# A decoder layer on one core: cross-attention scores from rounded keys and doubled queries

## What is computed

```
x = x + attn(layernorm(x))                        # Wq Wk Wv Wo, scores / 16
x = x + xattn(layernorm(x), ctx, mask)            # 77 keys, scores / 4, masked
x = x + ffn(layernorm(x))                         # 1024 slots
# xattn:
q = split(Q @ Wq.T + bq); k = split(K @ Wk.T + bk); v = split(V @ Wv.T + bv)
score = where(mask == 0, -inf, einsum('bhqd,bhkd->bhqk', q, k) * scale)
out   = einsum('bhqk,bhkd->bhqd', softmax(score), v)   ...   out @ Wo.T + bo
# ffn:
logits = xn @ se.T; dispatch = softmax over tokens; combine = softmax over slots
slots = dispatch.T @ xn; processed = gelu(slots @ w1) @ w2; out = combine @ processed
```

## Time and profile before

| | us |
|---|---|
| median of 3 runs (lowest, highest) | 1778.03 (1777.96, 1778.81) |
| profiled execution: its own time | 1779.52 |
| its span, first to last instruction | 1777.7 |
| one pass of the loop, of 13 | 105.37 |

### The profile page before, as it was taken

One profiled execution on the slowest core, in us unless ns is written; L12 is line 12 of the kernel. 1 busy time (PEld: TensorE's weight loads), 2 busy tenths in 40 slices (PEclk: granted clock), 3 DMA queues, 4 the chain that ended last, 5 costly groups with the idle time before them and its releaser, 6 DMA issues.

```text
span 1777.7 us, 40856 instructions
## 1 busy us (share of the span) xinstructions
PE 1739.7 (98%) x17306; PEld 1574.4 (89%) x17306; DVE 1161.5 (65%) x2307; ACT 1018.4 (57%) x1775; POOL 438.9 (25%) x351
## 2 busy tenths in 40 slices
PE   8899999999999999999999999999999999999998
PEld 7778898898989889898998989889898988989988
DVE  4657576676766668576675767667676666765453
ACT  4446566565565656556566656656656565655553
POOL 2103131322222223132222223222222213222232
PEclk9999999999999999999999999999999999999999
DMA  5000000000000000000000000000000000000000
GB/s 162 10 1 10 1 10 8 10 8 1 16 1 10 7 9 9 1 10 7 10 8 1 16 2 10 7 10 7 1 16 2 10 7 10 8 1 7 1 7 7
DMA packets 20853, 19.67 MB, mean 11 GB/s; under 512 B 9921, under 2 KB 19777, under 8 KB 20289
## 3 DMA queue, kind: packets, MB, share of 16 engines
q1 hardware_dynamic: 20672, 17.06, 3.5%
HBM read 12.86 MB, written 4.19 MB: 10 GB/s over the span
## 4 chain that ended last, share of the span: by engine, by line
PE 84%; ACT 5%; DVE 5%; issue 4%; POOL 2%; DMA 0%; POOLq 0%; SPq 0%; DVEq 0%; ACTq 0%
PE ps L465 21%; PE ps L466 19%; PE ps L467 19%; PE ps L590 3%; PE ps L573 2%; PE ps L553 2%; PE ps L775 2%; PE ps L700 2%; PE ps L620 2%; PE ps L843 1%; PE ps L665 1%; PE ps L766 1%; POOL h_lo L1446 1%; PE ps L872 1%; ACT L1034 1%
## 5 line engine op out<-in xcount | busy, mean ns | idle before, releaser
L1446 POOL TENSOR_TENSOR h_lo<-h_f,h_hi 128x512 fp32r<-128x512 f32 x256 | 336.8, 1323 | 1052.8 <-DVE h_hi L1329 1052.8
L465 PE MATMUL ps<-sl_hi,w_hi 128*128 128x256 f32 x1024 | 304.9, 298 | 5.4 <-DVE sl_lo L1088 2.9
L465 PE MATMUL ps<-w_hi,h_hi 128*128 128x256 f32 x1024 | 301.0, 294 | 5.5 <-POOL h_lo L1446 5.3
L466 PE MATMUL ps<-w_hi,h_lo 128*128 128x256 f32 x1024 | 290.1, 283 | 0.0
L467 PE MATMUL ps<-w_lo,h_hi 128*128 128x256 f32 x1024 | 289.9, 283 | 0.0
L466 PE MATMUL ps<-sl_hi,w_lo 128*128 128x256 f32 x1024 | 288.8, 282 | 0.0
L467 PE MATMUL ps<-sl_lo,w_hi 128*128 128x256 f32 x1024 | 288.7, 282 | 0.0
L465 PEld LDWEIGHTS ps<-sl_hi,w_hi 128*128 128x128 f32 x1024 | 194.4, 190 | 28.9 <-ACT h_f L1034 14.2
L1329 DVE CAST h_hi<-h_f 128x512 fp32r<-128x512 f32 x256 | 175.4, 691 | 67.0 <-ACT h_f L1034 66.2
L1034 ACT ACTIVATE h_f<-ps 128x512 f32<-128x512 f32 x256 | 151.2, 598 | 104.6 <-PE ps L467 103.6
L465 PEld LDWEIGHTS ps<-w_hi,h_hi 128*128 128x128 f32 x1024 | 196.2, 192 | 15.0 <-POOL h_lo L1446 11.3
(11 more groups left out here) (213 smaller groups left out, 4229.6 us busy)
## 6 DMA issues: line engine op xcount, KB each, us to landing
x<-in_x SPq DMA_DIRECT2D x16, 256.0 KB, 2.7
out<-acc SPq DMA_DIRECT2D x16, 256.0 KB, 2.2
g_w<-in_w SPq DMA_DIRECT2D x2, 1024.0 KB, 12.1
cx<-in_ctxT SPq DMA_DIRECT2D x16, 77.0 KB, 2.0
g_wqk<-in_wqk SPq DMA_DIRECT2D x1, 1024.0 KB, 6.4
g_se<-in_se SPq DMA_DIRECT2D x1, 1024.0 KB, 8.6
biases<-in_bias SPq DMA_DIRECT2D x1, 640.0 KB, 4.8
mk_i<-in_mask SPq DMA_DIRECT2D x16, 38.5 KB
```

The lines of the kernel that those rows point to most:

```text
L465: te.matmul(o, lhs[0], rhs[0], start=first, stop=False)
L466: te.matmul(o, lhs[1], rhs[0], start=False, stop=False)
L1446: Q_.tensor_tensor(h_lo[:, part, :], h_f[:, part, :], h_hi[:, part, :].bitcast(f32), ALU.subtract)\
```

## The change

Cross-attention scores are now made as self-attention's are. `kv` writes the keys once (`k2`, padded to 78 columns, the padding set to zero once). VectorE doubles them (`k2_d`, step `k2d`), ScalarE rounds them (`k2_hi`, step `k2h`), VectorE makes `k2_lo` (step `k2l`). The queries go through `q2d`, `q2h` and `q2s` the same way. `scores2` has 32 f32r products of 78 columns in place of 16 float32 ones of 77; `shifted2` has for each e eight f32r products in place of four float32 ones. The mask is 312 columns wide. To make room, `pt2` lies in the memory of `pt`: `before_in_pt` makes each Exp wait for the value product of the one before it in the ring. `g_se` moves to the memory where `g_wqk` was, so that its load waits until `wqk_lo` is made. GpSimd splits `w2` in four instructions instead of one. All tables of the order are new, and `START` has 224 idle products where it had 197.

```diff
+CP = 78
...
-    kv_ps=1, km2=1, v2_sb=1, mk=3, q2_ps=1, q2_sb=1,
+    kv_ps=1, k2_ev=1, k2_d=1, k2_h=1, k2_lo=1, v2_sb=1, mk=3, q2_ps=1, q2_ev=1, q2_d=1, q2_h=1, q2_sb=1,
...
@@ -46,34 +47,35 @@
 
 ORDER = dict(
-        m.lt.0 l.outer.3.0 d.kv m.dispatch.0 l.outer.3.1 c.xt.1 m.slots.0 l.comb.3 d.xt.2 c.k c.q d.q2 c.v
-        m.hidden.0.0 d.scores2.0 m.hidden.0.1 m.hidden.0.2 d.mt2.0 m.hidden.0.3 m.lt.1 l.combine.3 d.shifted2.0
...
+        m.lt.0 l.outer.3.0 d.kv m.dispatch.0 l.outer.3.1 c.xt.1 l.comb.3 m.slots.0 d.xt.2 c.k c.q d.q2 m.hidden.0.0
+        c.v m.hidden.0.1 m.hidden.0.2 d.scores2.0 m.hidden.0.3 m.lt.1 d.mt2.0 l.combine.3 d.shifted2.0 m.outer.0.0
...
-    d.kv c.xt1 d.xt2 d.q2 d.mt2.0 c.mt.0 d.pv2.0 d.mt2.1 c.pv.0 d.tr2.0 d.pv2.1 d.ob2.0 c.mt.1 d.tr2.1 c.pv.1 d.ob2.1
+    d.kv c.xt1 d.xt2 d.q2 d.mt2.0 c.mt.0 d.pv2.0 d.tr2.0 d.mt2.1 c.pv.0 d.ob2.0 d.pv2.1 c.mt.1 d.tr2.1 c.pv.1 d.ob2.1
...
-    "d.xt2": ("xt2_lo", 1), "c.xt1": ("xt1_lo", 1), "d.xt3": ("xt3_lo", 1), "d.kv": ("v2_sb", 1), "d.q2": ("q2_sb", 1),
+    "d.xt2": ("xt2_lo", 1), "c.xt1": ("xt1_lo", 1), "d.xt3": ("xt3_lo", 1), "d.kv": ("v2_sb", 1), "d.q2": ("q2_ev", 1),
...
+def before_in_pt(name, batch):
+
+    at = QUAD_USERS.index(f"{name[0]}{batch}{name[1:]}")
+    for token in reversed(QUAD_USERS[:at]):
+        head, step, *k = token.split(".")
+        if step in ("quad", "oct"):
+            return ("pv" if step == "quad" else "pv2", int(k[0]) + 1), int(head[1:])
+    return None
...
-        pt = sb("pt", [P, R, NT, S])
+        r_pt = region(8 * KB)
+        pt = at("pt", [P, R, NT, S], f32, r_pt)
...
-        km2 = sb("km2", [P, 2, C, CTX])
+        k2 = sb("k2", [P, C, CP])
+        r_q2s, r_k2l = region(4 * KB), region(4 * Q * CP)
+        q2_d, q2s = at("q2_d", [P, Q, S], f32, r_q2s), at("q2s", [P, Q, S], f32r, r_q2s)
+        k2_d, k2_lo = at("k2_d", [P, Q, CP], f32, r_k2l), at("k2_lo", [P, Q, CP], f32r, r_k2l)
+        k2_hi = sb("k2_hi", [P, Q, CP], f32r)
+        q2_hi = at("q2_hi", [P, Q, S], f32r, r_xd)
         v2z = sb("v2z", [CTX, H, VW])
-        r_pt2 = region(8 * KB)
-        pt2 = at("pt2", [CTX, R, 2, S], f32, r_pt2)
+        pt2 = at("pt2", [CTX, R, 2, S], f32, r_pt)
...
-        g_se = at("g_se", [P, NS, D], f32, r_pt2)
+        g_se = at("g_se", [P, NS, D], f32, r_lg)
...
-                    pe.wait_ge(s["km2"], nth("km2", a, 1))
+                    pe.wait_ge(s["k2_lo"], nth("k2_lo", a, 1))
                     pe.wait_ge(s["mk"], nth("mk", a, 3))
                 for i in range(R):
                     one = slice(32 * i, 32 * i + 1)
-                    te.matmul(ps[:, 1 + i, 0:4 * CTX], ones[one, :], mk_r[one, :, :].rearrange("p u c -> p (u c)"),
+                    te.matmul(ps[:, 1 + i, 0:4 * CP], ones[one, :], mk_r[one, :, :].rearrange("p u c -> p (u c)"),
                               start=True, stop=False)
                 for e in range(2):
                     for t in range(NT):
-                        at = (2 * e + t) * CTX
-                        for i in range(R):
-                            rows = slice(32 * i, 32 * i + 32)
-                            last = te.matmul(ps[:, 1 + i, at:at + CTX], q2[rows, c, t * P:(t + 1) * P],
-                                             km2[rows, e, c, :], start=False, stop=(e, t) == (1, NT - 1))
+                        at = (2 * e + t) * CP
+                        for keys, end in ((k2_hi, False), (k2_lo, (e, t) == (1, NT - 1))):
+                            for i in range(R):
+                                rows = slice(32 * i, 32 * i + 32)
+                                last = te.matmul(ps[:, 1 + i, at:at + CP], q2s[rows, 2 * c + e, t * P:(t + 1) * P],
+                                                 keys[rows, 2 * c + e, :], start=False, stop=end)
...
-                    for i in range(R):
-                        rows = slice(32 * i, 32 * i + 32)
-                        te.matmul(ps[0:CTX, 1 + i, e * S:(e + 1) * S], km2[rows, e, c, :], q2[rows, c, :],
-                                  start=True, stop=False)
+                    for keys, first in ((k2_hi, True), (k2_lo, False)):
+                        for i in range(R):
+                            rows = slice(32 * i, 32 * i + 32)
+                            te.matmul(ps[0:CTX, 1 + i, e * S:(e + 1) * S], keys[rows, 2 * c + e, 0:CTX],
+                                      q2s[rows, 2 * c + e, :], start=first, stop=False)
...
+                if n == 3:
+                    act.wait_ge(s["q2_sb"], nth("q2_sb", a, 1))
...
             def ex(a, n):
 
                 act.wait_ge(s["st_ps"], nth("st_ps", a, n + 1))
-                if n:
-                    act.wait_ge(s["pv"], nth("pv", a, n))
+                before = before_in_pt(f"c.quad.{n}", a)
+                if before:
+                    (signal, k), b = before
+                    act.wait_ge(s[signal], nth(signal, b, k))
...
             def q2_step(a):
 
                 act.wait_ge(s["q2_ps"], nth("q2_ps", a, 1))
+                if later(a):
+                    act.wait_ge(s["q2_d"], nth("q2_d", a - 1, 1))
                 for c in range(C):
                     last = nc.scalar.activation(q2[:, c, :], ps[:, 0, c * S:(c + 1) * S], ACT.Identity,
                                                 scale=XATTN_SCALE, bias=bcol[:, 2, c:c + 1])
-                last.then_inc(s["q2_sb"], 1)
+                last.then_inc(s["q2_ev"], 1)
+
+            def q2h_step(a):
+                act.wait_ge(s["q2_d"], nth("q2_d", a, 1))
+                copy(q2_hi[:, :, :], q2_d[:, :, :]).then_inc(s["q2_h"], 1)
+
+            def k2h_step(a):
+                act.wait_ge(s["k2_d"], nth("k2_d", a, 1))
+                copy(k2_hi[:, :, :], k2_d[:, :, :]).then_inc(s["k2_h"], 1)
...
             def ex2(a, c):
 
                 act.wait_ge(s["st2_ps"], nth("st2_ps", a, c + 1))
-                if not c and not later(a):
-                    act.wait_ge(s["i_sps"], 2 * ND)
-                if c:
-                    act.wait_ge(s["pv2"], nth("pv2", a, c))
+                before = before_in_pt(f"d.oct.{c}", a)
+                if before:
+                    (signal, k), b = before
+                    act.wait_ge(s[signal], nth(signal, b, k))
...
-                    for e in range(2):
-                        last = V.tensor_scalar(km2[:, e, c, :], ps[:, 0, D + c * CTX:D + (c + 1) * CTX],
-                                               half[:, e:e + 1], bk2m[:, e, c:c + 1], ALU.mult, ALU.add)
-                last.then_inc(s["km2"], 1)
+                    last = V.tensor_scalar(k2[:, c, 0:CTX], ps[:, 0, D + c * CTX:D + (c + 1) * CTX], bk2c[:, c:c + 1], None,
+                                           ALU.add)
+                last.then_inc(s["k2_ev"], 1)
                 V.tensor_tensor(v2z[:, :, 0:HD], ps[0:CTX, 0, 0:D].rearrange("p (h d) -> p h d", h=H),
                                 bv2[0:CTX, :].rearrange("p (h d) -> p h d", h=H), ALU.add).then_inc(s["v2_sb"], 1)
+
+            def q2d_step(a):
+
+                dve.wait_ge(s["q2_ev"], nth("q2_ev", a, 1))
+                if later(a):
+                    dve.wait_ge(s["st2_ps"], nth("st2_ps", a - 1, C))
+                twice(q2_d, q2).then_inc(s["q2_d"], 1)
+
+            def q2s_step(a):
+
+                dve.wait_ge(s["q2_h"], nth("q2_h", a, 1))
+                V.scalar_tensor_tensor(q2s[:, :, :], q2_hi[:, :, :].bitcast(f32), cols[:, NMASK:NMASK + 1], q2_d[:, :, :],
+                                       ALU.mult, ALU.add).then_inc(s["q2_sb"], 1)
+
+            def k2d_step(a):
+
+                dve.wait_ge(s["k2_ev"], nth("k2_ev", a, 1))
+                if later(a):
+                    dve.wait_ge(s["st2_ps"], nth("st2_ps", a - 1, C))
+                twice(k2_d, k2).then_inc(s["k2_d"], 1)
+
+            def k2l_step(a):
+                dve.wait_ge(s["k2_h"], nth("k2_h", a, 1))
+                minus(k2_lo[:, :, :], k2_d[:, :, :], k2_hi[:, :, :]).then_inc(s["k2_lo"], 1)
 
             def mask(a):
 
                 dve.wait_ge(s["mask_in"], nth("mask_in", a, 32))
                 if later(a):
                     dve.wait_ge(s["ex2"], nth("ex2", a - 1, C))
-                V.tensor_scalar(mk_r[:, :, :], mk_i[:, :].unsqueeze(1).broadcast_to([P, 2 * NT, CTX]), 0.0, MASKED,
+                V.tensor_scalar(mk_r[:, :, :], mk_i[:, :].unsqueeze(1).broadcast_to([P, 2 * NT, CP]), 0.0, MASKED,
...
             def mx2_step(a, c):
 
                 dve.wait_ge(s["s2_ps"], nth("s2_ps", a, c + 1))
-                V.tensor_reduce(mx2[:, c, :, :], ps[:, 1:1 + R, 0:4 * CTX].rearrange("p i (u c) -> p i u c", u=2 * NT), AX,
+                V.tensor_reduce(mx2[:, c, :, :], ps[:, 1:1 + R, 0:4 * CP].rearrange("p i (u c) -> p i u c", u=2 * NT)[:, :, :, 0:CTX], AX,
...
+            Q_.memset(k2[:, :, CTX:CP], 0.0).then_inc(s["i_vz"], 1)
+            Q_.memset(mk_i[:, CTX:CP], 0).then_inc(s["i_vz"], 1)
...
```

(6 more changed lines are left out.)

234 lines of the change are left out of this document (116 added, 118 removed).

## The result

The changed kernel takes 1796.53 us (median of 4 runs, 1795.63 to 1797.51) where the kernel before, on the same chip, takes 1778.42: a ratio of 1.0097, 95% interval 1.0085 to 1.0109. Predicted were 1770.9 us and 1761 to 1782. The profiled execution has a span of 1795.3 us, 17.6 more than before.

The account below looks back on a forecast made before the run. TensorE was taken to bound the kernel, busy 104.78 of 105.37 us a pass. Terms +0.6 - 11.2 + 7.0 - 3.5 = -7.1 us gave 1770.9 us on the median's scale, range 1761 to 1782.

Parts of the forecast that it names:

- Products: TensorE's cross-attention products: scores2 slightly dearer, +0.6 us in all; shifted2 0.35 us shorter, 32 times, -11.2 us.
- the +0.6 us in sum: scores2 on TensorE: eight sets at 0.12 us, 0.96 in place of 0.94, +0.02 each over 32.
- The rival with dear short products: In scores2, f32r products of 78 columns stream at four times their columns: +7.7 us, 1778.0 us; 12 in 100.
- Queries in time: Ahead of scores2.0: the new query chain ends within 0.1 us of being wanted, cost 0, without margin.
- The late-queries rival: Query sum or shuffle loses 1.0 us a pass, delaying scores2.0: +13 us in the loop, 1783.9 us; 13 in 100.
- the 3.2 us of added VectorE work: New shuffles, sum and low part per batch, on VectorE's 72.07 us a pass: as a sum they cost nothing.
- The next link: From second maxima transposes to shifted2.0: VectorE 0.2 us late, set against the 0.18 wait for `h_lo` that goes: 0.
- Since TensorE has no slack in the loop, 26 of the 32 count in full: Of 32 savings of 0.35 us in shifted2, the loop's 26 count fully: -9.1 to -11.2 us, -11.2 taken.
- Prologue: Before the loop: +7.0 us of waiting allowed by added idle products, -3.5 us from the earlier `xh_a`.
- The 7.0 us of idle products: In the prologue, 27 more idle products on TensorE at 0.26 us each mean +7.0 us more waiting.
- The closed waits: Rival: the new order also closes TensorE's remaining loop waits, 0.59 plus about 0.2 us a pass, -10, 1761 us; 15 in 100.

Follow-up runs that it names:

- i_narrow_q2: Changed kernel with the new VectorE and ScalarE steps on q2 done on 32 of 256 columns from the second batch on; 1794.87 us, 1.0090.
- o_old_products_moves: Products and probability tiles of the kernel before, run in the order of j_both; 1788.52 us, 1.0054.
- j_both: c_bias_back with second-half steps reordered on VectorE and ScalarE, and the first hidden group's last high part made on ScalarE; 1774.69 us, 0.9975.
- c_bias_back: Changed kernel with the bias of x1 on GpSimd put back ahead of the hidden layer's four low parts; 1786.99 us, 1.0038.
- d_keep_later: Changed kernel with VectorE's copy of the residual moved from ahead of the second shift to behind the MoE accumulation; 1795.42 us, 1.0088.
- b_old_tables: Changed kernel's products and tiles in the order tables and rings of the kernel before, six new steps put in; 1860.83 us, 1.0456.

## Why the prediction was wrong

- **Products: right.** A scores2 takes 1.18 us, so the +0.6 us in sum didn't come; a shifted2 takes 0.87 against 0.92 predicted. The rival with dear short products is out: eight sets of 78 columns pass in 0.96 us (473.94 to 474.90).
- **Queries in time: right**, and with more margin than predicted: `q2s` ends at 473.33, scores2.0 starts at 473.72. The late-queries rival is out; `q2s` took 1.28 us in the mean, 1.29 at most. That the 3.2 us of added VectorE work cost nothing was right as well (i_narrow_q2, o_old_products_moves).
- **The next link: the step that failed.** The prediction put 0.2 us of new wait in front of shifted2.0 and set it against the 0.18 for `h_lo`: 0. Measured are 0.54 us more from combine.3 to shifted2.0 (2.14 to 1.60). The term that was mis-sized is one of the three operations of 0.4 to 0.7 between maximum and shift: the last cast, 0.97 beside GpSimd's low part. By the rows (an estimate, see j_both) that is about 0.44 of the 0.54, and the chain without it 0.1. The 0.18 for `h_lo` did go, as predicted, but it doesn't cover 0.54. And this was the only link that was followed. The four others, behind `k_lo` and behind the copy of the residual, weren't looked for; together the new order costs 1.40 us a pass, 18 us.
- **"Since TensorE has no slack in the loop, 26 of the 32 count in full": failed with it.** It holds for the mended order (0.75 us a pass), not for one in which VectorE is late in the same stretch: 0.16 of 0.75 arrived.
- **The order was read for what each step waits for, not for what runs beside it.** The prediction knew that both engines lengthen each other, priced that for `q2s`, and found GpSimd idle there. It didn't ask where the bias of x1 had gone: beside `k_lo`, whose row said 1211 to 2316 ns. That is 0.88 us a pass (c_bias_back). Nor what the residual's copy, put ahead of the shift, meets: a low part, 1.51 us instead of 0.52 in d_keep_later (1.12 in the kernel before).
- **Prologue: half right.** `xh_a` took 0.73 us and its transposes started at 68.06 instead of 72.01, 4 us where 3.5 were predicted. The 7.0 us of idle products weren't paid: 0.7 in sum where +3.5 was predicted. They fill a wait that is there anyway; their number doesn't say how much longer it is. In the kernel before TensorE was also busy throughout at a granted clock of 0.56 behind the wait for `xh_a` (72.00 to 78.00), which the prediction didn't count; the changed kernel has 1.00 there. What ate these gains, no run took apart.
- **The closed waits, in part.** The prediction held against this rival that the place of the largest wait, for `edt`, kept its neighbours. In the kernel before TensorE waits there 13 times, 3.1 us in all; in the changed kernel's loop no wait for it shows. The new waits outweigh it.

By pass: order +1.40, products -0.16 in place of -0.75: 1.24. With the prologue's 0.7 and the epilogue's 1.1 that is the 17.6 us of the spans, to 0.3 us. Of the five distances in the trace after (1.8 us) and the two shorter shifted2 (0.65 and 0.15, with the waits behind them), 0.2 us a pass remain: a balance of smaller changes, the wait for `edt` among them, that I haven't followed one by one.

## What to carry to other kernels

When a step moves on a second engine, list what will run beside it and what is queued behind each of the two. Where one engine's instruction only ends when its neighbour's does, starting it earlier gains nothing; what stands behind it must go ahead of it, or the neighbour elsewhere. Moving it to a third engine helps only if it doesn't stand there in front of the next link of the same chain. And a saving on the bounding engine counts only in stretches where no other engine is the later one: measure the distance between two of its steps, one on each side of the saving, not its busy time.

## What the runs showed of the hardware

- VectorE's cast of 512 elements a partition takes 0.42 us alone and 0.84 to 1.44 in the rows read here beside GpSimd's subtraction of 1.28; `k_lo` 1.21 and 2.32; the copy of the residual 0.52 and 1.51; `qs` 1.27 and 2.31. The shift (0.73 to 0.75) and `cm` (0.69), which read `ps`, stay as short beside it. GpSimd pays too: the bias 1.29 and 2.29.
- The lengths add up as if one engine stood still until the other is done. In the changed kernel the bias is given from 479.96, while `qs` runs to 481.1; 1.1 of waiting and its own 1.29 are 2.4, the row says 2.29. `k_lo` is given from 481.02, the bias ends at 482.25; 1.2 of waiting and its own 1.21 are 2.4, the row says 2.32. The Trainium skill, page SBUF — State Buffer, section Who interferes with whom, has this rule: casts and copies in VectorE's two-port modes, and its instructions with two SBUF inputs, lock GpSimd's reads out and are locked out by them for a whole instruction; one SBUF input beside PSUM is free of it. The rows here agree to 0.15 us, by the numbers above and by the casts that end 0.27 and 0.28 us behind GpSimd, where 0.42 alone would be due. The prediction drew on it for `q2s` only.
- In b_old_tables each wait of 2.8 us, in a pass whose other waits are at most 0.44, was followed by a lower granted clock: 0.55 over the next 6.9 us in the pass shown, 0.75 in the one behind it. The waits of up to 0.5 us in the loops of all other kernels never were: their passes show 1.00.
- f32r products of 78 columns in four row tiles cost per set what those of 256 columns do, 0.12 us, and what f32 products of 77 columns do per set of records.
